# A transformer layer on one core: four f32 projections as three f16 products each, and a Hadamard rotation of half sums

## The reference

```python
def layer(x, Wq, Wk, Wv, Wo, W_down_kv, W_up_k, W_up_v, ffn_weight):   # x: 32 x 512 x 256, f32
    a = layernorm(x)
    q = a @ Wq
    latent = (a @ Wk + a @ Wv) @ W_down_kv          # 64 wide
    k, v = latent @ W_up_k, latent @ W_up_v         # 16 heads of 16
    scores = clip(q k^T / 16) * exp(-1e-4 * |i - j|)
    x1 = x + layernorm((softmax(scores) @ v) @ Wo)
    xh = layernorm(x1) @ H                          # H: 256x256 Hadamard / 16
    xq = clip(round(xh / s), -8, 7) * s             # s = max|xh| of a token / 7
    return x1 + layernorm(xq @ ternary(ffn_weight)^T)
```

## Time and profile before

| | |
|---|---|
| median of 3 runs | 1436.95 us (1436.71 to 1436.96) |
| profiled execution, first to last instruction (its span) | 1433.2 us |
| one pass of the loop in it | 41.83 us |
| busy in the span: PE, DVE, ACT, POOL | 94%, 82%, 77%, 58% |
| TensorE clock granted, mean | 0.983 of full speed |

### The profile page before, as it was taken

One profiled execution on the slowest core, in us unless ns is written; L12 is line 12 of the kernel. 1 busy time (PEld: TensorE's weight loads), 2 busy tenths in 40 slices (PEclk: granted clock), 3 DMA queues, 4 the chain that ended last, 5 costly groups with the idle time before them and its releaser, 6 DMA issues.

```text
span 1433.2 us, 35971 instructions
## 1 busy us (share of the span) xinstructions
PE 1349.5 (94%) x12330; PEld 600.5 (42%) x12330; DVE 1179.9 (82%) x2739; ACT 1098.2 (77%) x1125; POOL 834.7 (58%) x1238
## 2 busy tenths in 40 slices
PE   5889999999999999999999999999999999999863
PEld 3334444444444444444444444444444444443332
DVE  7567888888888888888888888888888888888655
ACT  1878787888888788878878887887888787787831
POOL 4223655666565666556557655656765655675446
PEclk9999999999999999999999999999999999999986
DMA  6455456556555645656564565655556555555420
GB/s 194 154 167 170 154 172 202 155 164 206 164 182 173 197 156 166 206 157 190 173 190 157 173 201 157 193 175 187 156 177 194 163 185 184 176 156 175 128 77 31
DMA packets 174557, 241.45 MB, mean 168 GB/s; under 512 B 28336, under 2 KB 145200, under 8 KB 174512
## 3 DMA queue, kind: packets, MB, share of 16 engines
q1 hardware_dynamic: 140176, 206.78, 46.5%
q10 hardware_dynamic: 34336, 34.08, 7.7%
HBM read 154.80 MB, written 69.21 MB: 156 GB/s over the span
## 4 chain that ended last, share of the span: by engine, by line
PE 76%; DVE 8%; issue 5%; ACT 4%; DMA 3%; SPq 2%; POOL 2%; DVEq 0%; ACTq 0%; POOLq 0%
PE heads_ps L720 27%; PE scores_ps L707 16%; PE misc_ps L603 8%; PE misc_ps L635 7%; PE misc_ps L660 4%; PE misc_ps L614 3%; PE misc_ps L587 3%; ACT probs L909 2%; DVE x_hl L1204 2%; PE misc_ps L595 2%; PE misc_ps L678 2%; DVE diagonal L1253 2%; DVE weighted L1161 2%; PE misc_ps L625 2%; PE misc_ps L669 1%
## 5 line engine op out<-in xcount | busy, mean ns | idle before, releaser
L909 ACT ACTIVATE probs<-scores_ps 128x1024 f32<-128x1024 f32 x768 | 759.8, 1026 | 248.0 <-PE scores_ps L707 247.9
L720 PE MATMUL heads_ps<-probs,v_sb 128*32 128x512 f32 x4096 | 525.4, 603 | 3.6 <-DVE heads L1150 1.9
L1253 DVE TENSOR_TENSOR diagonal<-scores_ps,comp 128x1024 f32<-128x1024 f32 x256 | 312.2, 1219 | 70.1 <-PE scores_ps L707 70.1
L707 PE MATMUL scores_ps<-q_rep,k_rep 64*128 64x128 f16 (+2 forms) x5120 | 324.6, 251 | 16.0 <-DVE diagonal L1253 9.2
L707 PEld LDWEIGHTS scores_ps<-q_rep,k_rep 64*128 64x128 f16 x5120 | 165.6, 94 | 348.7 <-DVE diagonal L1253 149.5
L916 ACT ACTIVATE probs<-diagonal 128x2048 f32<-128x2048 f32 x128 | 246.0, 1922 | 0.0
L996 POOL TENSOR_TENSOR ln_neg_mean<-zero,ln_moments 128x4 f32<-128x4 f32 (+1 forms) x131 | 34.6, 264 | 356.5 <-DVE ln_moments L1115 356.3
L1161 DVE SCALAR_TENSOR_TENSOR weighted<-misc_ps,edges 128x384 f32<-128x384 f32 x256 | 129.4, 547 | 64.3 <-PE misc_ps L603 33.8
L720 PEld LDWEIGHTS heads_ps<-probs,v_sb 128*32 128x32 f32 x4096 | 91.5, 108 | 171.7 <-issue 169.8
L1038 POOL TENSOR_TENSOR q_hl<-weighted,q_hl 128x768 f16<-128x768 f32 x64 | 105.5, 1648 | 77.5 <-DVE q_hl L1168 77.5
L1043 POOL TENSOR_TENSOR heads_c<-heads_c,den_spread 128x1024 f32<-128x1024 f32 (+1 forms) x33 | 75.7, 2296 | 111.0 <-DMA den_spread<-den_scratch 111.0
(11 more groups left out here) (132 smaller groups left out, 1511.5 us busy)
## 6 DMA issues: line engine op xcount, KB each, us to landing
q_rep<-q_scratch SPq DMA_DIRECT2D x128, 384.0 KB, 4.3
k_rep<-k_scratch SPq DMA_DIRECT2D x256, 192.0 KB, 3.9
q_scratch<-q_hl SPq DMA_DIRECT2D x64, 384.0 KB, 2.6
k_scratch<-k_hl SPq DMA_DIRECT2D x64, 384.0 KB, 3.1
x_in<-in_L_attn_x_dram ACTq DMA_DIRECT2D x32, 512.0 KB, 4.9
heads_c<-heads SPq DMA_DIRECT2D x256, 64.0 KB, 2.5
x_res<-in_L_attn_x_dram ACTq DMA_DIRECT2D x32, 512.0 KB, 6.8
den_spread<-den_scratch SPq DMA_DIRECT2D x256, 64.0 KB, 2.3
```

The source lines that it names most:

```text
L707: ins = mm(scores_ps[:, place + par, at:at + n * P], k_rep[rows, pair, kv_, k_cols], q_rep[rows, pair, qv_, q_cols], start=True, stop=True)
L720: ins = mm(heads_ps[W32 * g:W32 * (g + 1), :], v_sb[:, b.slot, kt, at:at + W32], probs[:, quad % 2, g, kt, :], start=(kt == 0), stop=(kt = ...
L909: nc.scalar.activation(flat[:, :, at:at + S], scores_ps[:, place:place + 2, :], ACT.Exp, scale=EXP_SCALE).then_inc(off_probs, 1)
L1253: v.tensor_tensor(diagonal[:, quad % 2, 2 * two:2 * two + 2, :], scores_ps[:, place:place + 2, :], comp[:].rearrange("p t n -> p (t n)").u ...
```

## The change

1. The f32 products of q, latent, k and v become f16 ones. Each operand is held as a high f16 half and a low one (the rest), weights times 1024, and high x high, high x low and low x high are summed in PSUM (`PRODUCTS`). The factor is taken out where DVE reads q, k and v anyway.
2. The high halves of xT and latT are made by ACT (`x_high_take`, `lat_high_take`), the low ones by DVE as a difference, in the place of its copies.
3. The rotation: H of 256 is [[G, G], [G, -G]] with G 128x128, so POOL makes the sum and the difference of the two channel halves of x1 before it normalises them, and PE multiplies each transposed half with G alone: 128 columns for 256, as many products.
4. The opening prepares the f16 weights (ACT, DVE, POOL) and bounds two more of them for the choice of the path.
5. The loops are placed so that their first instruction begins an instruction block (`head_slot`). The tables carry each step's group in themselves; the order of the steps that existed is the same.

```diff
 SCALAR_STEPS = {
-    4: [("load_res", 0)], 12: [("x1T", 0)], 14: [("x1T", 1)], 15: [("load_x", 0)], 21: [("round_x", 0)],
-    22: [("round_x", 1), ("round_x", 2), ("round_x", 3)], 30: [("qintT", 0)],
+    4: [("load_res", 0, "a"), ("xT", 0, "pre")], 6: [("xT", 1, "pre")], 9: [("lat", 0, "pre")], 12: [("x1T", 0, "b")], 14: [("x1T", 1, "b")],
+    15: [("load_x", 0, "load")], 21: [("round_x", 0, "b")], 22: [("round_x", 1, "b"), ("round_x", 2, "b"), ("round_x", 3, "b")],
+    30: [("qintT", 0, "b")],
 }
...
+PRODUCTS = ((0, 0), (0, 1), (1, 0))
 
...
             return ver, slice(at, at + tiles * P)
 
-        wq = sb("wq", [P, DC, D])
+        wq_hl = sb("wq_hl", [P, 2, DC, D], F16)
         wo = sb("wo", [P, DC, D])
-        w_down = sb("w_down", [P, DC, LAT])
-        w_lat = sb("w_lat", [P, DC, LAT])
-        w_up_k = sb("w_up_k", [P, D])
-        w_up_v = sb("w_up_v", [P, D])
+        w_lat_hl = sb("w_lat_hl", [P, 2, DC, LAT], F16)
+        w_up_k_hl = sb("w_up_k_hl", [P, 2, D], F16)
+        w_up_v_hl = sb("w_up_v_hl", [P, 2, D], F16)
...
-            with eng.Fori(0, (B - 6) // 2) as loop:
+            with nc.Fori(0, (B - 6) // 2, engines=[eng.engine], head_slot={eng.engine: 0}) as loop:
```

The stages on PE (k and v are changed in the way of q):

```diff
-                for c in range(DC):
-                    for half in range(2):
-                        ins = mm(misc_ps[LAT * half:LAT * (half + 1), bank, 0:S // 2], w_lat[:, c, :],
-                                 xT[:, c, half * S // 2:(half + 1) * S // 2], start=(c == 0), stop=(c == DC - 1))
+                if b.buffers == 1:
+                    for c in range(DC):
+                        for half in range(2):
+                            ins = mm(misc_ps[LAT * half:LAT * (half + 1), bank, 0:S // 2], w_lat[:, c, :],
+                                     xT[:, c, half * S // 2:(half + 1) * S // 2], start=(c == 0), stop=(c == DC - 1))
+                else:
+                    for c in range(DC):
+                        for n, (wh, xh) in enumerate(PRODUCTS):
+                            for half in range(2):
+                                ins = mm(misc_ps[LAT * half:LAT * (half + 1), bank, 0:S // 2], w_lat_hl[:, wh, c, :],
+                                         xT_hl[:, xh, c, half * S // 2:(half + 1) * S // 2], start=(c == 0 and n == 0),
+                                         stop=(c == DC - 1 and n == len(PRODUCTS) - 1))
                 ins.then_inc(in_psum["lat"], 1)
...
-                ins = mm(misc_ps[:, BANK["q", part], :], wq[:, piece, part * P:(part + 1) * P], xT[:, piece, :],
-                         start=(piece == 0), stop=(piece == DC - 1))
+                if b.buffers == 1:
+                    ins = mm(misc_ps[:, BANK["q", part], :], wq[:, piece, part * P:(part + 1) * P], xT[:, piece, :],
+                             start=(piece == 0), stop=(piece == DC - 1))
+                else:
+                    for n, (wh, xh) in enumerate(PRODUCTS):
+                        ins = mm(misc_ps[:, BANK["q", part], :], wq_hl[:, wh, piece, part * P:(part + 1) * P], xT_hl[:, xh, piece, :],
+                                 start=(piece == 0 and n == 0), stop=(piece == DC - 1 and n == len(PRODUCTS) - 1))
                 if piece == DC - 1:
                     ins.then_inc(in_psum["q"], 1)
...
                     for c in range(DC):
                         for hl in range(2):
-                            ins = mm(tokens(bank)[:, n, :], x1_hl[:, hl, c, t * P:(t + 1) * P], hadamard[:, c, :],
-                                     start=(c == 0 and hl == 0), stop=(c == DC - 1 and hl == 1))
+                            ins = mm(tokens(bank)[:, n, c * P:(c + 1) * P], x1_hl[:, hl, c, t * P:(t + 1) * P], hadamard[:],
+                                     start=(hl == 0), stop=(hl == 1))
                 ins.then_inc(in_psum["xh"], 1)
```

The takes on ACT and DVE, and the rotation on POOL:

```diff
+            def x_high_take(b, part):
+                act.wait_ge(in_psum["xT"], part_count("xT", b, part))
+                nc.scalar.activation(xT_hl[:, 0, part, :], misc_ps[:, BANK["xT", part], :], ACT.Copy).then_inc(x_high, 1)
+
+            def lat_high_take(b, part):
+                act.wait_ge(in_psum["lat"], part_count("lat", b, 0))
+                nc.scalar.activation(latT_hl[:, 0, :], misc_ps[:, BANK["lat", part], 0:S // 2], ACT.Copy).then_inc(lat_high, 1)
+
...
-                v.tensor_copy(xT[:, part, :], misc_ps[:, BANK["xT", part], :]).then_inc(taken["xT"], 1)
+                bank = misc_ps[:, BANK["xT", part], :]
+                if b.buffers == 1:
+                    v.tensor_copy(xT[:, part, :], bank).then_inc(taken["xT"], 1)
+                    return
+                dve.wait_ge(x_high, part_count("xT", b, part))
+                v.tensor_tensor(xT_hl[:, 1, part, :], bank, xT_hl[:, 0, part, :], ALU.subtract).then_inc(taken["xT"], 1)
...
-                    ins = v.tensor_copy(dst, src)
+                    if b.buffers == 1:
+                        ins = v.tensor_copy(dst, src)
+                    else:
+                        ins = v.tensor_scalar(dst, src, 1.0 / W_GAIN ** 2, None, ALU.mult)
...
+                pool.wait_ge(x1_ready, b.done)
+                first, second = x1[:, b.slot, b.rows, 0:P], x1[:, b.slot, b.rows, P:D]
+                nc.gpsimd.tensor_tensor(x1n[:, b.rows, 0:P], first, second, ALU.add)
+                nc.gpsimd.tensor_tensor(x1n[:, b.rows, P:D], first, second, ALU.subtract)
                 rstd(3, b)
                 for t in b.tiles:
-                    ins = nc.gpsimd.tensor_scalar(x1n[:, t, :], x1[:, b.slot, t, :], m["neg_mean"][:, t:t + 1], m["rstd"][:, t:t + 1],
-                                                  ALU.add, ALU.mult)
+                    nc.gpsimd.tensor_scalar(x1n[:, t, 0:P], x1n[:, t, 0:P], m["neg_mean"][:, t:t + 1], m["rstd"][:, t:t + 1], ALU.add, ALU.mult)
+                    ins = nc.gpsimd.tensor_scalar(x1n[:, t, P:D], x1n[:, t, P:D], m["rstd"][:, t:t + 1], 0.0, ALU.mult, ALU.add)
                 ins.then_inc(x1n_ready, 1)
```

The opening on POOL, and then on ACT:

```diff
                 x_apply(b)
+                pool.wait_ge(second_loaded, 16 * SECOND)
+                for w, up in enumerate((w_up_k, w_up_v)):
+                    nc.gpsimd.tensor_scalar(sq_up[:, w, :], up, W_GAIN, 0.0, ALU.mult, ALU.add).then_inc(w_scaled, 1)
+                pool.wait_ge(w_scaled, 2)
+                pool.wait_ge(w_high, 3)
+                for w, up_hl in enumerate((w_up_k_hl, w_up_v_hl)):
+                    nc.gpsimd.tensor_tensor(up_hl[:, 1, :], sq_up[:, w, :], up_hl[:, 0, :], ALU.subtract).then_inc(w_low, 1)
+                pool.wait_ge(w_low, 2)
+                for w, up in enumerate((w_up_k, w_up_v)):
+                    ins = nc.gpsimd.tensor_tensor(sq_up[:, w, :], up, up, ALU.mult)
+                ins.then_inc(w_squared, 1)
...
+                nc.scalar.dma_start(wq, Wq.rearrange("(c p) n -> p c n", p=P)).then_inc(second_loaded, 16)
                 act.wait_ge(second_loaded, 16 * SECOND)
-                nc.scalar.activation(squares[:, 0], wq[:], ACT.Square)
+                nc.scalar.activation(wq_hl[:, 0], wq, ACT.Copy, scale=W_GAIN).then_inc(w_high, 1)
+                for up, up_hl in ((w_up_k, w_up_k_hl), (w_up_v, w_up_v_hl)):
+                    nc.scalar.activation(up_hl[:, 0, :], up, ACT.Copy, scale=W_GAIN).then_inc(w_high, 1)
                 load_x(b.other(1), 0)
+                for part in range(2):
+                    x_high_take(b, part)
+                nc.scalar.activation(squares[:, 0], wq, ACT.Square)
+                lat_high_take(b, 0)
```

197 lines of the change are left out of this document (123 added, 74 removed), and 15 rows, old and new, of tables (TENSOR_CLOSING, TENSOR_STEPS).

## The result

The changed kernel takes **1516.84 us** (median of 4 runs, 1514.69 to 1517.53) where the kernel before, on the same chip, takes 1436.95 (1436.71 to 1438.15): a ratio of 1.055, 95% interval 1.0535 to 1.0565. It is 80 us slower; the forecast was some 13 us faster. The profiled execution spans 1514.3 us.

A forecast was written before the change was run, and what follows sets the result against it. PE was taken to set the pass, with DVE equally binding in its first half. Over 29 passes -14.5 us, opening +0.5 and closing +1.2 gave 1424 us; forecast case 1414 to 1433, whole range 1398 to 1446.

The forecast's parts named there:

- POOL's adds could also slow DVE: Beside the rotation's sum and difference, DVE runs no cast; slowdown taken as nothing, 0.3 us at most.
- moved DVE by 0.65 us there: At step 16, scores start 0.5 us later and DVE takes the diagonal behind them 0.65 us late.
- Net: 0.5 us a pass: Whole pass: 0.5 us saved, the other stages' savings eaten by the hand-off; -14.5 us over 29 passes.
- Products on PE: q, latent, k, v and xh stages on PE get shorter, 2.7 us a pass in sum; q stage 1.38 us.
- Hand-off: Ahead of DVE's first xT take: DVE idles 1.25 us a pass (0.9 to 1.6) for ACT's high half behind `load_res`.
- from there to the end of the pass DVE and ACT have room, so it stays: Second half of the pass: the 0.53 us saved on q's second part is kept.
- Rotation: On POOL: adds of 2.5 us cost nothing, eight normalisings take 2.8 us, x1n 0.6 us later; 0.3 us shows at x1T.
- The slower rival: At x1n: eight POOL instructions over 3.3 us (0.41 each) make PE wait; 1438 to 1450 us, up to 1462; chance 0.15.
- Opening and closing: Ends of the kernel: weight checks add 0.5 us (0 to 2), the last batch's POOL work 1.2 (0 to 3).
- Loops: Loop alignment: nothing to gain but 13 x 0.02 us.
- the DVE wait: Sign: DVE waits 1.0 to 1.4 us for ACT ahead of the first take of xT in each pass.
- the PE gaps ahead of steps 6, 7 and 11: Sign: PE gaps of some 2 us a pass, ahead of steps 6, 7, 11 and 18.

The follow-up runs named there:

- `e_act2`: Changed kernel, hand-off as in the change, with the casts of both second parts (k, q) on ACT: 1457.57 us, ratio 1.0131.
- `e_align`: Kernel before with only the change's placing of the loops: 1434.56 us, ratio 0.9996.
- `e_order`: Changed kernel with POOL taking k's first split ahead of `add_out`, no instruction added: 1480.35 us, ratio 1.0304.
- `e_norot_hand3`: Changed kernel with the rotation undone and the high half of xT's first part made at step 3, ahead of `load_res`: 1504.46 us, ratio 1.0467.
- `e_best`: Changed kernel with xT's first high half at step 3, k's second cast on ACT, POOL's second k split ahead of `heads_normalize`: 1441.66 us, ratio 1.0051.
- `e_delay`: Kernel before with one small extra DVE reciprocal (0.49 us) ahead of k's second part: 1498.62 us, ratio 1.0443.
- `e_hand3`: Changed kernel with ACT making the high half of xT's first part at step 3, ahead of `load_res`: 1474.96 us, ratio 1.0258.

## Why the prediction was wrong

**The step that failed** is one sentence: "POOL's adds could also slow DVE ... I take nothing, 0.3 us at most". I looked only at the *new* adds (sum and difference), saw no cast beside them, and asked nothing of the *old* POOL instructions that the change would move against DVE's. The rule was in the text; it was applied to the wrong instructions. The hint was in the earlier trace rows, the same cast of q at 0.91 and 0.56 us, and I took it as 0.3 us at most. The rows of before that would have shown it are the cast at 638.59 and the add at 638.79, and the two at 174.92 and 175.24 above: a blocked cast of k and its price, 1.7 us a pass, stood in the trace that the forecast was made from. In the change the runs put it at 1.87 us a pass, 54 of the 93 us by which the forecast missed. The forecast itself moved DVE by 0.65 us there; a lead of 0.20 us could not be taken to last.

**The net of the rest** was a second error, "Net: 0.5 us a pass". The forecast of 41.3 us a pass has its match in `e_act2`, the change with nothing blocked: 42.53, 0.7 more than before in place of 0.5 less, or some 36 us over 29 passes. At 1457.57 us (ratio 1.0131) it is slower than the kernel before, so the direction would have been wrong without the blocked cast too. Term by term:
- *Products on PE.* The stages came out as worked out: q 1.40 us (1.38 forecast; 1.91 in the earlier trace rows). Two rows of the chain:

```profile
235.88 1.40 PE misc_ps L636 x6
280.31 1.40 PE misc_ps L636 x6
```

  The price from the rows before held (229 ns a product forecast, 233 measured). The Trainium skill's 131 ns ("TensorE: Matmul & The Clock Gate", Back-to-back issue gap) would make the stage 0.79 us, and the trace does not agree: 1.40. But PE's busy time fell by 2.13 us a pass (41.41 to 39.28), not 2.7. By the distances between starts the changed stages are 2.6 us shorter, so the forecast of the stages was right; of the rest, 0.2 to 0.3 us is scores and products of probabilities and v that take longer, the remainder I haven't placed.
- *Hand-off.* The mechanism and the size were right: DVE waits 1.37 us for 1.25 forecast. ACT, then DVE:

```profile
656.29 0.38 ACTq L939 DMA_DIRECT2D x_res<-in_L_attn_x_dram  x1
656.80 0.60 ACT L925 ACTIVATE xT_hl<-misc_ps 128x512 f16<-128x512 f32 x1 [0.51 <-issue]
```

```profile
657.50 0.69 DVE L1217 TENSOR_TENSOR xT_hl<-misc_ps,xT_hl 128x512 f16<-128x512 f32 x1 [1.37 <-ACT xT_hl L925]
```

  It costs 1.29 us a pass, almost all of itself. The savings behind it did not make it good: even with the hand-off at step 3 the products make the pass 0.02 us longer, and the waits that eat PE's saving are for exponentials. "from there to the end of the pass DVE and ACT have room, so it stays" (of q's second part) is the step that failed here: ACT's share was taken from its busy time, and PE waits for ACT all the same.
- *Rotation.* 0.61 us saved a pass with its POOL costs in. POOL's eight instructions take 3.45 us, 0.43 each, for 2.8 forecast; PE waits 0.62 us for x1n at x1T for 0.3 forecast. The slower rival's condition (over 0.41) was met, with that mechanism worth some 0.3 us a pass: not the cause.

```profile
663.30 0.45 POOL L1104 TENSOR_SCALAR y_sb<-y_sb,ln_neg_mean,ln_rstd 128x128 f32<-128x128 f32 x1
663.73 0.37 POOL L1105 TENSOR_SCALAR y_sb<-y_sb,ln_rstd 128x128 f32<-128x128 f32 x1
...
666.06 0.69 POOL L1105 TENSOR_SCALAR y_sb<-y_sb,ln_rstd 128x128 f32<-128x128 f32 x1
```

- *Opening and closing.* +0.5 us (0 to 2) and +1.2 (0 to 3) were forecast. The four products, the comparison and the reduction of the opening were priced from no row. Measured, the second latent is taken at 48.81 us for 43.42, 5.4 later; it is at 47.4 to 49.5 in every kernel with the f16 products and the latent's halves in their place, and at 43.1 to 45.2 in those without. What costs it there stays open. Behind the last latent it is +3.3 us.
- *Loops.* Nothing, as forecast (`e_align`).

Of the signs that the prediction named, the DVE wait, the q stage and the PE gaps ahead of steps 6, 7 and 11 appeared; the gap ahead of step 18 did too, but at 2.19 us and for a reason that wasn't in the text; the pass of 41.3 us did not. The only slower rival ran through x1n and stopped at 1462 us; one on the lead of k's cast over the add, at +1.9 us a pass, would have stood near 1480 from the forecast's own sum.

## What to carry to other kernels

When a change shifts two engines against each other, list the instructions of DVE from SBUF to SBUF (casts, copies, two SBUF inputs) and the long POOL instructions near them, with the lead of one over the other; a lead of tenths of a microsecond is a debt. Look for a group whose longest is far over its shortest: in a steady loop the same cast at 0.56 and 2.44 us is a wait that no column of waits shows. It is cheaper to take such a cast off DVE, to ACT or out of PSUM, than to tune the order: the two best kernels here (1417.78 us with the f32 products and the rotation, 1418.95 with the f16 products) both do that, while moves in the order made another instruction late: `e_order` the casts of q, `e_norot_hand3` the cast of k, `e_best` the 4-column product in some passes.

## What the runs showed of the hardware that I had not expected

- A DVE cast of 768 columns from SBUF takes 0.56 us, and 2.44 to 2.58 when a POOL add of 2.35 us started 0.2 to 0.3 us before it. ACT's cast of the same data beside the same add takes 0.83 us, and DVE's weighing from PSUM isn't lengthened.
- It isn't a matter of size: a DVE product of 4 columns with both inputs in SBUF took 1.48 us behind POOL's split, and 2.33 in one pass of `e_delay`, for 0.13.
- It goes both ways: POOL's last half-width instruction above takes 0.69 us for 0.37, since DVE's cast of q runs from 665.92 to 666.51.
- Once the order has turned, the cost is the same in pass after pass (2.44 to 2.46 us in 28 batches of the changed kernel), or it comes by turns, as in `e_hand3`; it doesn't average out.
- Behind the 2.2 us wait of PE that follows a blocked cast the granted clock fell to 0.50 for some 3.3 us in four passes of the changed kernel, and such passes took 45.6 to 46.3 us for 44.4.
